# Half-width delta levels, window scores in four array quarters, four-column GLA sums and a redrawn order, in a two-layer FP32 kernel

## The reference, cut to what matters

```
# local attention, per window of 64 queries: scores of 8 heads against this window and the one before
sim = jnp.einsum('bhwid,bhwjd->bhwij', bq, bk)

# gla: one state row per key channel, summed over the 16 key channels by the query
S = jnp.exp(gt)[..., None] * S + kt[..., None] * vt[..., None, :]
ot = jnp.einsum('bhk,bhkv->bhv', qt, S)

# delta rule: the inverse of a unit lower triangular 32x32 matrix, per chunk, head and beta
def inv_body(T, i):
    row = T[..., i, :]
    new = row + jnp.einsum('...k,...kc->...c', row, T)
```

## Time and profile before

| what | value |
|---|---|
| median of 3 executions | 1432.37 us (1429.29 to 1435.21) |
| profiled execution | 1425.25 us |
| its span, first to last instruction | 1423.9 us |
| PE busy / PEld busy | 1298.2 us (91%) / 1026.1 us (72%) |
| DVE / ACT / POOL busy | 1038.2 (73%) / 739.3 (52%) / 675.1 us (47%) |
| DMA | 231.46 MB, 163 GB/s on average |

### The profile page before, as it was taken

How to read it: one execution, slowest core, us unless ns; L and a number is a source line. 1 busy time by engine, 2 the same in 40 slices (tenths; PEclk the granted TensorE clock), 3 DMA queues, 4 the chain that set the end, 5 groups by cost and what they waited for, 6 DMA issues and landing times.

```text
span 1423.9 us, 42901 instructions
## 1 busy us (share of the span) xinstructions
PE 1298.2 (91%) x18034; PEld 1026.1 (72%) x18034; DVE 1038.2 (73%) x1974; ACT 739.3 (52%) x2084; POOL 675.1 (47%) x549
## 2 busy tenths in 40 slices
PE   5777789898999899999999899999999999989997
PEld 3445577776777678777788777777777878877785
DVE  4787898875788677777677877987598855765444
ACT  4777676445645466445665356734665244422221
POOL 3464466465465343556447445564536444422600
PEclk9998899999999999999999999999999999999999
DMA  5101165533565346445566555664645745656645
GB/s 195 49 16 49 39 231 168 190 127 104 170 211 177 130 157 189 150 159 173 168 202 214 168 167 153 205 194 138 177 145 176 230 169 183 222 176 200 215 142 173
DMA packets 90719, 231.46 MB, mean 163 GB/s; under 512 B 9376, under 2 KB 15648, under 8 KB 90400
## 3 DMA queue, kind: packets, MB, share of 16 engines
q1 hardware_dynamic: 90384, 228.12, 49.2%
q10 hardware_dynamic: 144, 0.59, 0.1%
HBM read 225.53 MB, written 3.15 MB: 161 GB/s over the span
## 4 chain that ended last, share of the span: by engine, by line
PE 58%; DVE 9%; issue 3%; DMA 2%; ACT 1%; DVEq 0%; ACTq 0%
PE bank L954 12%; PE bank L907 12%; PE bank L818 8%; PE bank L944 3%; PE bank L925 3%; PE bank L607 3%; DMA ogate<-gates 2%; PE bank L639 2%; PE bank L935 2%; PE bank L697 2%; PE bank L918 2%; DVE ogate L1377 1%; PE bank L751 1%; PE bank L661 1%; PE bank L673 1%
## 5 line engine op out<-in xcount | busy, mean ns | idle before, releaser
L1771 POOL TENSOR_TENSOR vgate<-vgate,xT 128x1024 f32<-128x1024 f32 x128 | 309.3, 2420 | 172.3 <-DMA vgate<-gates 172.3
L954 PE MATMUL bank<-ogate,wo 128*128 128x256 f32 x1024 | 248.7, 386 | 8.7 <-DVE ogate L1377 6.9
L907 PE MATMUL bank<-wv,vgate 128*128 128x128 f32 x2048 | 254.9, 278 | 1.8 <-DVEq L1391 0.9
L907 PEld LDWEIGHTS bank<-wv,vgate 128*128 128x128 f32 x2048 | 244.1, 193 | 15.1 <-issue 7.3
L954 PEld LDWEIGHTS bank<-ogate,wo 128*128 128x128 f32 x1024 | 189.3, 191 | 41.8 <-issue 17.8
L1377 DVE TENSOR_TENSOR ogate<-ogate,bank 128x1024 f32<-128x1024 f32 x128 | 154.5, 1209 | 17.5 <-DMA ogate<-gates 9.6
L1717 POOL TENSOR_TENSOR rot<-rot 128x512 f32<-128x512 f32 x64 | 83.3, 1301 | 98.8 <-DVE rot L1051 98.7
L1734 POOL TENSOR_TENSOR kv<-kv,gqk 128x512 f32<-128x512 f32 x64 | 84.9, 1327 | 94.6 <-DVE kv L1131 94.6
L1729 POOL TENSOR_TENSOR prob<-prob,rsum 128x256 f32<-128x256 f32 (+1 forms) x64 | 62.6, 978 | 137.6 <-DVE rsum L1075 137.6
L1488 ACT ACTIVATE prob<-prob,mx 128x128 f32<-128x128 f32 (+1 forms) x256 | 95.9, 377 | 54.7 <-DVE mx L1072 54.5
L1131 DVE TENSOR_TENSOR_SCAN kv<-ge,kv 128x256 f32<-128x256 f32 x128 | 115.0, 939 | 1.2 <-DVE ogate L1377 0.5
(11 more groups left out here) (236 smaller groups left out, 2682.3 us busy)
## 6 DMA issues: line engine op xcount, KB each, us to landing
vgate<-gates SPq DMA_DIRECT2D x128, 512.0 KB, 4.0
ogate<-gates SPq DMA_DIRECT2D x128, 512.0 KB, 4.0
wv<-in_wv_moe SPq DMA_DIRECT2D x128, 256.0 KB, 4.3
wo<-in_wo_moe SPq DMA_DIRECT2D x128, 256.0 KB, 4.5
kv<-values SPq DMA_DIRECT2D x128, 128.0 KB
local<-in_local SPq DMA_DIRECT2D x1, 1715.0 KB, 9.6
wqkv<-in_wqkv SPq DMA_DIRECT2D x2, 768.0 KB, 6.5
x<-in_x SPq DMA_DIRECT2D x8, 128.0 KB, 7.7
```

Of the source, the lines that this page charges most:

```text
L907: i = nc.tensor.matmul(out[:, n * D:(n + 1) * D], xg[:, e, n * P:(n + 1) * P], m.wv[slot][:, e, :], start=(q, n, e) == (0, 0, 0), stop=(q, ...
L954: i = nc.tensor.matmul(out[:, 0:T], m.wo[slot][:, e, :], cg[:, e, :], start=(h, q, e) == (0, 0, 0), stop=(h, q, e) == (MH - 1, 1, EQ - 1))
L1771: tt(gate, gate, spread(m.xT[b % 2][:, :], 1, EQ), ALU.mult).then_inc(s.vgated, 1)
```

## The change

Four things are changed together.

Delta levels: a level changes only the columns whose bit i is zero, 16 of 32. `lev` now streams those columns of `winv` alone, `pmat` has 16 columns, `levmul` streams 16, and `levmask` and `levadd` handle 256 elements per partition and not 512; the mask constant is cut likewise.

Window scores: the 8 matmuls go to all four 64x64 quarters. Two quarters with the same output rows have different contraction rows, and these write different banks, so `lscore` takes two banks; VectorE's `score` reads them with two instructions. The order of heads in `prob` changes, and `pv` follows it.

GLA sums: `gsum` runs once per four value columns, with a matmul in each of the four column strips, after both `kv` buffers of these columns are ready. There are four `kv` buffers and not three, and their loads come in pairs.

Order: all turn strings and the bank string are drawn anew (one line shown).

```diff
@@ -54,8 +54,9 @@
     out["eye"] = r == c
     out["below"] = c < r
     out["upper"] = c >= r
-    out["level_neg"] = -1.0 * np.concatenate(
-        [(r // (2 * s) == c // (2 * s)) & (r // s % 2 == 1) & (c // s % 2 == 0) for s in (1, 2, 4, 8, 16)], axis=1)
+    level = lambda s, c: (r // (2 * s) == c // (2 * s)) & (r // s % 2 == 1) & (c // s % 2 == 0)
+    upper = lambda s: c[:, c[0] // s % 2 == 0]
+    out["level_neg"] = -1.0 * np.concatenate([level(1, c)] + [level(s, upper(s)) for s in (2, 4, 8, 16)], axis=1)
 
 TENSOR_TURNS = (
-    "aaaaaaaaabbaabbbGGGbbGXabbaaabbbcGcGaaccaaGabbcaGbabaabbbabbGaabGbabaacaGbbacGGbbcGcGGGcbbGbbaababbbcGcaacGcGc"
-    "aaabbGzaGbabbCabbCGAbbFGbaabaAbcCcaaccGGcaaaVbbVGAzaAbAGGGGVPAPaVbbbbVabAVbaAbbCAabCAVcaFGacFPAaPAAGaAcbVbFaVa"
...
 def gla_ticks(b):
-    ticks = [[("gv", b)], [("gqk", b)] + [("kvload", b, j) for j in (0, 2, 4)], [("gz", b)]]
+    ticks = [[("gv", b)], [("gqk", b)] + [("kvload", b, j) for j in (0, 2, 4, 6)], [("gz", b)]]
     for j in range(0, GJ, 2):
-        ticks += [[("gkv", b, j)], [("gmul", b, j)] + ([("gsum", b, j - 2)] if j else []) +
-                  ([("kvload", b, j + 4)] if 2 <= j < GJ - 4 else [])]
-    return ticks + [[("gsum", b, GJ - 2), ("gg", b)], [("gnorm", b)], [("grms", b)], [("gadd", b)]]
+        ticks += [[("gkv", b, j)], [("gmul", b, j)] + ([("gsum", b, j - 4)] if j and j % 4 == 0 else []) +
+                  ([("kvload", b, j + k) for k in (4, 6) if j + k < GJ] if j and j % 4 == 0 else [])]
+    return ticks + [[("gsum", b, GJ - 4), ("gg", b)], [("gnorm", b)], [("grms", b)], [("gadd", b)]]
 
 
...
-BANKS = {"xnT": 1, "proj": 1, "projv": 1, "qkT": 1, "lscore": 1, "probT": 1, "pv": 1, "wo": 1, "lnorm": 1,
+BANKS = {"xnT": 1, "proj": 1, "projv": 1, "qkT": 1, "lscore": 2, "probT": 1, "pv": 1, "wo": 1, "lnorm": 1,
...
@@ -439,7 +441,7 @@
 def kv_of(b, j):
     i = (b * GJ + j) // 2
-    return i % 3, i // 3 + 1
+    return i % 4, i // 4 + 1
 class Memory(Named):
...
-        sb("kmat", NC_, CH), sb("kT", NC_, CH), sb("winv", NG, CH), sb("winvT", NG, CH), sb("pmat", NG, CH)
+        sb("kmat", NC_, CH), sb("kT", NC_, CH), sb("winv", NG, CH), sb("winvT", NG, CH), sb("pmat", NG, CH // 2)
...
@@ -624,20 +626,25 @@
 
     def lscore(b, l, w):
 
-        bank, keys = banks.of("lscore", b, l, w), keys_of(w)
-        out, qk = take(bank), m.qkT[place(b, l) % 2]
+
+        both, keys = [banks.of("lscore", b, l, w, i=r) for r in range(2)], keys_of(w)
+        for bank in both:
+            take(bank)
+        qk = m.qkT[place(b, l) % 2]
         for n in range(last_projected(w) + 1):
             for k in range(2):
                 t = banks.of("qkT", b, l, n, k)
                 pe.wait_ge(t.emptied, t.use)
-        for c in range(LH // 2):
-            for r in range(2):
-                rows = slice(r * LD, (r + 1) * LD)
+        for i in range(LH // 4):
+            for r, half in ((0, 0), (1, 1), (0, 1), (1, 0)):
+                rows, c = slice(r * LD, (r + 1) * LD), 2 * i + half
                 k = qk[rows, 1, c, max(w - 1, 0) * WIN:(w + 1) * WIN]
                 if swapped(w):
                     k = k.rearrange("p (a t) -> p a t", a=2)[:, ::-1, :]
-                last = nc.tensor.matmul(out[rows, c * keys:(c + 1) * keys], qk[rows, 0, c, w * WIN:(w + 1) * WIN], k, start=True, stop=True)
-        last.then_inc(bank.filled, 1)
+                last = nc.tensor.matmul(both[r].ap[half * WIN:(half + 1) * WIN, i * keys:(i + 1) * keys],
+                                        qk[rows, 0, c, w * WIN:(w + 1) * WIN], k, start=True, stop=True)
+                if i == LH // 4 - 1 and half == 1 - r:
+                    last.then_inc(both[r].filled, 1)
 
     def probT(b, l, w):
         bank, keys = banks.of("probT", b, l, w), keys_of(w)
                 last = nc.tensor.matmul(out[r * LD:(r + 1) * LD, c * WIN:(c + 1) * WIN], values[0:keys, 2 * c + r, :],
-                                        probT_of(m, b, l, w)[0:keys, c, r * WIN:(r + 1) * WIN], start=True, stop=True)
+                                        probT_of(m, b, l, w)[0:keys, 2 * r + c // 2, c % 2 * WIN:(c % 2 + 1) * WIN], start=True, stop=True)
         last.then_inc(bank.filled, 1)
 
...
     def gsum(b, j):
         bank = banks.kept("gla_sum", b)
         out = take(bank)
-        pe.wait_ge(s.gmul, nth("gmul", b, j))
-        kv = m.kv[kv_of(b, j)[0]]
-        for i in range(2):
-            strip, at = divmod(j + i, 4)
-            last = nc.tensor.matmul(out[at * 32:(at + 1) * 32, 0:T], m.gla_sum[:, strip, :], kv[:, i, :], start=strip == 0, stop=strip == 3)
-        last.then_inc(bank.filled if j == GJ - 2 else s.gsum, 1)
+        pe.wait_ge(s.gmul, nth("gmul", b, j + 2))
+        for i in range(4):
+            kv = m.kv[kv_of(b, j + i // 2 * 2)[0]]
+            last = nc.tensor.matmul(out[i * 32:(i + 1) * 32, 0:T], m.gla_sum[:, j // 4, :], kv[:, i % 2, :], start=j == 0, stop=j == GJ - 4)
+        last.then_inc(bank.filled if j == GJ - 4 else s.gsum, 1)
 
     def lev(b, i):
         bank = banks.kept("masked", b, i)
-        out = split(take(bank), n=NC_)
+        out = split(take(bank)[:, 0:NC_ * CH], n=NC_)
         pe.wait_ge(s.winvT, nth_winvT(b, i))
-        w4 = m.winv[:, :, :].rearrange("p (a c) t -> p a c t", a=2)
+        w4 = upper_columns(m.winv[:, :, :], i)
         for c in range(NC_):
-            last = per_head(out[:, c, :].rearrange("p (a t) -> p a t", a=2), m.kT[:, c, :], w4[:, :, c, :], start=True, stop=True)
+            last = per_head(out[:, c, :].rearrange("p (a n t) -> p a n t", a=2, t=2 ** i), m.kT[:, c, :], w4[:, c::NC_, :, :], start=True, stop=True)
         last.then_inc(bank.filled, 1)
 
     def levmul(b, i):
         bank, masked = banks.kept("level", b, i), banks.kept("masked", b, i)
-        out = split(take(bank), n=NG)
+        out = split(take(bank)[:, 0:NG * CH // 2], n=NG)
...
+def upper_columns(winv, i):
+    size = 2 ** i
+    return winv.rearrange("p g (n a c) -> p g n a c", a=2, c=size)[:, :, :, 0, :]
...
         reduce(rn, split(m.ssq[u % 2][:, :], n=LH), AX.X, ALU.add).then_inc(s.ssum, 1)
 
     def score(b, l, w):
-        bank, keys = banks.of("lscore", b, l, w), keys_of(w)
-        top, rsum = sums_of(m, b, l, w)
+        keys, (top, rsum) = keys_of(w), sums_of(m, b, l, w)
         p = prob_of(m, b, l, w)[:, :, 0:keys]
-        out = split(filled(bank)[:, 0:LH // 2 * keys], n=LH // 2)
         v.wait_ge(s.loaded_local, 16)
         v.wait_ge(s.sexp, nth("score", b, l, w) - 4)
         before = window_before(b, l, w, 3)
         if before:
             read = banks.of("probT", *before)
             v.wait_ge(read.filled, read.fill)
-        tt(p, spread(band_of(m, w), 1, LH // 2), out, ALU.subtract).then_inc(bank.emptied, 1)
-        v.wait_ge(bank.emptied, bank.use)
+        for r in range(2):
+            bank = banks.of("lscore", b, l, w, i=r)
+            out = split(filled(bank)[:, 0:LH // 4 * keys], n=LH // 4)
+            tt(p[:, 2 * r:2 * r + 2, :], spread(band_of(m, w), 1, LH // 4), out, ALU.subtract).then_inc(bank.emptied, 1)
+        for r in range(2):
+            bank = banks.of("lscore", b, l, w, i=r)
+            v.wait_ge(bank.emptied, bank.use)
         reduce(top[:, :], p, AX.X, ALU.min).then_inc(s.smin, 1)
         yield
         v.wait_ge(s.sexp, nth("score", b, l, w))
 
     def levmask(b, i):
         bank = banks.kept("masked", b, i)
-        out = filled(bank)
+        out = filled(bank)[:, 0:NC_ * CH]
+        at = CH + (i - 1) * CH // 2
         tt(m.pmat[:, :, :].rearrange("p (a c) t -> p c a t", a=2), out.rearrange("p (c a t) -> p c a t", c=NC_, a=2),
-           spread(spread(m.level_neg[:, i * CH:(i + 1) * CH], 1, 2), 1, NC_), ALU.mult).then_inc(bank.emptied, 1)
+           spread(spread(m.level_neg[:, at:at + CH // 2], 1, 2), 1, NC_), ALU.mult).then_inc(bank.emptied, 1)
 
     def levadd(b, i):
         bank = banks.kept("level", b, i)
-        out = filled(bank)
-        tt(m.winv[:, :, :], m.winv[:, :, :], split(out, n=NG), ALU.add).then_inc(bank.emptied, 1)
+        w = upper_columns(m.winv[:, :, :], i)
+        tt(w, w, filled(bank)[:, 0:NG * CH // 2].rearrange("p (g n t) -> p g n t", g=NG, t=2 ** i), ALU.add).then_inc(bank.emptied, 1)
 
     def dT(b):
         before = banks.kept("level", b, 4)
         sp.wait_ge(s.gv_sent, 16 * (b + 1))
-        i = (b * GJ + j) // 2 - 3
+        i = (b * GJ + j) // 2 - 4
         if i >= 0:
-            before, at = divmod(i, GJ // 2)
-            if at == GJ // 2 - 1:
+            before, at = divmod(i // 2, GJ // 4)
+            if at == GJ // 4 - 1:
                 o = banks.kept("gla_sum", before)
                 sp.wait_ge(o.filled, o.fill)
             else:
-                sp.wait_ge(s.gsum, before * (GJ // 2 - 1) + at + 1)
```

More of the change, by code:

```diff
@@ L150 @@
+    "44034043014304306")
 PACKS = {
@@ L156 @@
     "layer1": {"w_delta": (P, 3, D), "conv": (P, 3, CONV), "w_gate": (P, 4, P), "gate_b": (P, 2), "dnorm": (P, CH), "wo_delta": (P, D),
[L157 removed]
```

(5 more changed lines are left out.)

111 lines of the change are left out of this document (56 added, 55 removed).

## The result

The changed kernel is a little slower: a median of 1441.2 us (1428.92 to 1451.24) over 20 executions beside 1435.22 us over 20 of the kernel before, a ratio of 1.0039 (95% interval 1.0020 to 1.0058). It had been forecast at 1397 us, with a range of 1370 to 1420. That of before took 1425.25 us, 10 us less than its median, and that of after 1435.15 us, 6 us less; their mean granted clocks of 0.980 and 0.952 stand beside medians over the executions of 0.974 and 0.950.

The account below looks back on a forecast made before the run. TensorE, busy 1298 of 1424 us, was taken to set the time. Steps save 54.4 us gross, 19.4 are given back, net 35: 1432.4 - 35 = 1397 us median, range 1370 to 1420.

Parts of the forecast that it names:

- The steps' own savings: On TensorE: scores 24.3, GLA sums 17.9, lev 12.2 us, levmul no gain; gross 54.4 us.
- The quarters and strips do not take turns: Denies a rival (0.13) on scores: quarters take turns, scores save nothing, 1418 us; with strips taking turns too, 1431 us.
- What is given back: Part of the gross saving lost again through front, instructions and order: 19.4 us in all, leaving net 35 us.
- (a): First 200 us: half of the 7.6 us that 18 scores save there counted as lost, 3.8 us.
- (b): Delta levels: about 12 instruction stops in or behind a lev lengthen by its 0.38 us, 4.6 us.
- (c): New order: less room between steps that hand out work and take it back; 9 us at ogate, 2 elsewhere, 11 us.
- Behind 200 us almost every microsecond saved on TensorE counts: After the first 200 us TensorE, busy 1151 of 1224 us, was taken to set the time.
- the new order costs more than the steps save: Rival at the ogate buffer: 1 us lost per each of 64 heads, 64 against 54.4 saved, 1442 us; chance 0.07.
- idle time behind 200 us passes 110: Sign that the prediction is wrong: TensorE's idle time after the first 200 us, 73 us before, exceeds 110 us.
- TensorE's idle time: Sign over the whole span: span less TensorE's busy time should rise from 126 to some 140 us.
- mask and add: VectorE's levmask and levadd: levmask falls from 689 to about 414 ns, levadd as well; 17.6 us less.
- the reads: VectorE's score in two instructions, 2 x 414 for 674 ns, 0.15 us more each; 9.9 us more over 64.

Follow-up runs that it names:

- old_levels: The kernel before with the narrow lev, levmul, levmask and levadd alone, in the old order; median 1436.83 us, ratio 1.0022.
- old_all: The kernel before with levels, GLA sums and four-quarter scores all changed, in the old order with the bank string redrawn; median 1435.71 us, ratio 1.0008.
- new_order_old_widths: The changed kernel with its order, banks and GLA sums, but full-width levels and scores in two opposite quarters; median 1453.19 us, ratio 1.0143 to the kernel before.

## Why the prediction was wrong

**The steps' own savings** were right: 56.7 us measured, 54.4 forecast, with `levmul` at 1.19 us, so 16 streamed columns cost what 32 do. The Trainium skill, TensorEngine Tiling (Array Packing), Instruction Overhead, says that a matmul of one column takes as long as one of 60. From 32 to 16 columns this trace agrees; from 64 to 32 it does not, since `lev` fell from 1.03 to 0.69 us. The quarters and strips do not take turns.

**"What is given back"** is the step that failed: 19.4 us stood there, 66 were measured. (a) The front: 3.8 us forecast; there the other waits grew by 5.7 us and the clock fell from 0.92 to 0.85. (b) Instructions: 4.6 us forecast, 11.8 measured. The wait was the right one, its size was not: it was reckoned for `lev` alone, but every step made shorter means that a packet of 256 is used up sooner, and old_levels has 8 us more of these stops. (c) The order: 11 us. As waits the size is near (16 us behind 200 us), as a cause it is wrong. Only 3 of the 16 us are waits of the product, where (c) had them. And old_all, in the old order, has 67.2 us of such idle time behind 200 us, more than the changed kernel's 55.5. There the levels and sums added some 5 us, banks and reads some 10 and the quarters some 13, so short steps bring waits without a new order. By the ratios above, the order itself costs some 4 us with all parts and some 20 with the old widths.

**The clock had no term** at all: 33 us between the two profiled executions, and some 28 by my estimate from the medians of the clock (0.974 and 0.950). The earlier trace rows showed 0.980 and 0.92, and I took TensorE's durations as fixed. The clock fell 12 times in the span of before and 26 times in that of after, each time behind a stretch in which TensorE stood idle for a part, so more idle time seems to cost twice. Of the 78 us more at 1.2 GHz (58 and 136 in the traces), 31 lie in the front, and 31 come right behind a stop for instructions (14 us before, 44 after). The products in the front raise the clock in all four settings, but pay in two.

**"Behind 200 us almost every microsecond saved on TensorE counts"** is wrong by the three runs that left work out of the kernel before, and by old_levels: 60% in scores and expert products, none in narrower levels, 190% where the instructions go too. TensorE is busy for 94% of that stretch, but this does not make it the only bound: TensorE's waits for other engines grew by 9 us with half the scores and by 26 with three experts of four, and its wait for instructions by 8 with the narrow levels.

**The rivals.** That the new order costs more than the steps save had 0.07 and is the side on which it ended, but not by its mechanism: waits for VectorE at the product L960 are 7.8 and 4.1 us. The sign "idle time behind 200 us passes 110" would not have caught it either (102 us), since it doesn't see the clock. TensorE's idle time was to be 140 us and is 160, VectorE's busy time 1030 and is 996: mask and add saved 17.0 us as forecast, the reads cost 4 and not 9.9 (411 ns each, but 96 of them occupy 35.5 us, as they overlap), and the scans took 105 us and not 115.

**Open** is why the fast quarters pay nothing while leaving out as much work pays 14 us. The shared mark of what paid little (narrow levels, quarters) is that as many instructions run in less time, and of what paid well that instructions go; the stops agree in direction, but at 4 to 11 us are too small to be all of it.

## What to carry to other kernels

Where the engine with 91% is fed by chains through others, leave out some of its work first and see what the time does: here the price of a microsecond was 0.6, 0, or 1.9 by the kind of step. Write the granted clock as a term: here it fell with shorter steps beside longer waits. Count instructions too: where TensorE ran through a packet of 256 in under 5 us, it stopped for the next in more than half of the cases (22 of 40 before, 28 of 43 after). Small matmuls gained by fewer instructions, and not by fewer columns.

## What the hardware showed that was not expected

- TensorE stops up to 5.2 us inside a step whose data is all there, always at the same place in each 256 of its instructions (474 stops in 20 traces). Of the 94 packets that the kernel before takes over 6 us to run through, one ends in a stop. 4096 instructions fewer took away 23 of 29 us of this in the levels.
- A matmul of 32x32 tiles with 16 columns takes as long as one with 32 (1.19 and 1.22 us per 64).
- Four 64x64 quarters work at once (0.60 us for 1.02), and four 128x32 strips take the time of two (0.57 and 0.56 us).
- Products that nobody reads, put in the front, go with a kernel 0.5 to 0.7% faster in two of four settings; the two intervals of the smaller one touch.
- VectorE's scan, not touched, went from 939 to 862 ns in the mean. That goes with the order: 855 ns in new_order_old_widths, 968 in old_all. The median is 681 and 680 ns. What changed is the number of long scans, over 900 ns: 32 of 128 before, 24 after. GpSimd was at work for 77% of a long scan's time in both traces, and for 8% and 5% of the others'. The group in the changed kernel and in new_order_old_widths:

```profile
L1146 DVE TENSOR_TENSOR_SCAN kv<-ge,kv 128x256 f32<-128x256 f32 x128 | 105.1, 862 | 2.5 <-DVE ogate L1393 1.0 <-ACT ge L1568 0.4 <-DVE kv L1139 0.3
```

```profile
L1139 DVE TENSOR_TENSOR_SCAN kv<-ge,kv 128x256 f32<-128x256 f32 x128 | 104.2, 855 | 2.2 <-DVE ogate L1385 1.0 <-ACT ge L1560 0.4
```
